# Causal mask by VectorE instead of a matmul, and sixteen biased exponentials for each of two sequences

## The reference

```python
x1 = x + attn(cond(x, labeler))           # cond: x @ W.T plus a low-rank term, chosen by a label per sequence
# attn: 32 heads of 32, 8 key/value heads, each shared by 4 heads
qkv = h @ w_qkv.T + b_qkv
q, k = apply_rope(q), apply_rope(k)
scores = einsum('bhqd,bhkd->bhqk', q, k) / sqrt(32)
scores = where(tril(ones(64, 64)), scores, -1e20)
attn = softmax(scores, axis=-1)
out = einsum('bhqk,bhkd->bhqd', attn, v) @ w_o.T + b_o
out2 = x1 + ffn(cond2(x1, language))      # two routed low-rank projections
```

## Time and profile before

| what | value |
|---|---|
| median of 3 runs | 1226.75 us (1225.2 to 1227.36) |
| span of the profiled execution | 1224.6 us |
| median less that span | 2.15 us |
| TensorE busy | 1199.6 us, 98% of the span |
| VectorE, ScalarE, GpSimd busy | 602.9, 379.0, 303.9 us |
| mean granted TensorE clock | 0.999 of full speed |

### The profile page before, as it was taken

How to read it: one execution, slowest core, us unless ns; L and a number is a source line. 1 busy time by engine, 2 the same in 40 slices (tenths; PEclk the granted TensorE clock), 3 DMA queues, 4 the chain that set the end, 5 groups by cost and what they waited for, 6 DMA issues and landing times.

```text
span 1224.6 us, 20268 instructions
## 1 busy us (share of the span) xinstructions
PE 1199.6 (98%) x7424; PEld 1071.1 (87%) x7440; DVE 602.9 (49%) x1173; ACT 379.0 (31%) x1157; POOL 303.9 (25%) x182
## 2 busy tenths in 40 slices
PE   7999999999999999999999999999999999999997
PEld 7999988888888888888889998888888888888886
DVE  5222136767676766777773226344443333334443
ACT  4212124455545555555543224111111111111110
POOL 0000123433433344444220002222222222222220
PEclk9999999999999999999999999999999999999999
DMA  6111032111111111110312314111111111111100
GB/s 245 35 36 51 9 121 82 44 47 56 43 48 46 43 43 43 43 52 25 119 54 87 108 70 139 53 59 59 52 51 51 51 51 51 51 51 51 51 35 34
DMA packets 30003, 74.82 MB, mean 61 GB/s; under 512 B 4114, under 2 KB 8722, under 8 KB 29970
## 3 DMA queue, kind: packets, MB, share of 16 engines
q1 hardware_dynamic: 29970, 74.36, 17.6%
HBM read 57.57 MB, written 16.78 MB: 61 GB/s over the span
## 4 chain that ended last, share of the span: by engine, by line
PE 93%; DVE 3%; ACT 1%; DMA 1%; issue 1%; POOL 0%; SPq 0%; DVEq 0%; ACTq 0%
PE psum L949 21%; PE psum L368 21%; PE psum L1499 19%; PE psum L1454 14%; PE psum L984 4%; PE psum L1012 4%; PE psum L1471 2%; PE psum L997 2%; PE psum L1479 2%; PE psum L968 1%; PE psum L1487 1%; PE psum L979 1%; PE psum L1029 1%; ACT low L738 1%; DVE rot_t L801 1%
## 5 line engine op out<-in xcount | busy, mean ns | idle before, releaser
L368 PE MATMUL psum<-c_high_low,w_h 128*128 128x256 f32 (+1 forms) x1344 | 238.4, 288 | 9.6 <-ACT w_h L242 8.1
L368 PEld LDWEIGHTS psum<-c_high_low,w_h 128*128 128x128 f32 x1344 | 205.0, 193 | 10.0 <-DVE c_high_low L296 8.1
L1499 PE MATMUL psum<-fr_h,c_high_low 128*128 128x512 f32 (+1 forms) x768 | 212.6, 361 | 0.1
L949 PE MATMUL psum<-p_h,c_high_low 128*128 128x512 f32 (+1 forms) x768 | 196.4, 359 | 0.5 <-DVE qkv L906 0.5
L368 PE MATMUL psum<-c_high_low,w_l 128*128 128x256 f32 (+1 forms) x704 | 177.8, 279 | 2.1 <-DVE w_l L350 2.1
L1454 PE MATMUL psum<-w_h,c_high_low 128*128 128x512 f32 x512 | 170.2, 397 | 0.8 <-DVE w_l L1279 0.8
L1499 PEld LDWEIGHTS psum<-fr_h,c_high_low 128*128 128x128 f32 x768 | 136.5, 188 | 22.6 <-issue 0.3
L949 PEld LDWEIGHTS psum<-p_h,c_high_low 128*128 128x128 f32 x768 | 134.1, 189 | 13.4 <-issue 0.7
L1499 PE MATMUL psum<-fr_l,c_high_low 128*128 128x512 f32 (+1 forms) x384 | 138.3, 360 | 0.0
L368 PEld LDWEIGHTS psum<-c_high_low,w_l 128*128 128x128 f32 x704 | 127.6, 193 | 2.3 <-DVE w_l L350 2.3
L1337 POOL TENSOR_TENSOR x_out<-x,spare 128x1024 f32<-128x1024 f32 x16 | 38.8, 2423 | 350.3 <-DMA out<-x_out 331.4
(11 more groups left out here) (142 smaller groups left out, 1996.5 us busy)
## 6 DMA issues: line engine op xcount, KB each, us to landing
ring<-in_x_t SPq DMA_DIRECT2D x32, 256.0 KB, 2.7
attn_scratch<-ring SPq DMA_DIRECT2D x16, 512.0 KB, 2.6
ring<-attn_scratch SPq DMA_DIRECT2D x32, 256.0 KB, 2.8
ring<-in_x_tok SPq DMA_DIRECT2D x16, 512.0 KB, 3.3
out<-x_out SPq DMA_DIRECT2D x16, 512.0 KB, 3.2
ring<-in_wqkv_t SPq DMA_DIRECT2D x12, 512.0 KB, 4.5
ring<-in_last_t SPq DMA_DIRECT2D x10, 512.0 KB, 4.8
w_raw<-in_w_cond SPq DMA_DIRECT2D x8, 512.0 KB, 9.4
```

What stands on the lines that cost most here:

```text
L368: mm = pe.matmul(to, stationary, moving, start=start and n == 0, stop=k == KT - 1 and n == len(passes) - 1, skip_group_check=True)
L949: mm = pe.matmul(to, sx[:, k, :], moving(w, n, k), start=first, stop=False, skip_group_check=True)
L1499: mm = pe.matmul(b_ps[:, n, 0:cols.stop - cols.start], s[:, k, :], w[:, k, cols], start=first, stop=n == 2 and k == KT - 1 and s is x1t_l)
```

## The change

VectorE now masks while it moves the scores out of PSUM: one `scalar_tensor_tensor` writes `-SCALE * scores - hidden`, where `hidden` (new, 128x64) holds 0 or -1e20, so hidden places come out at +1e20. A minimum over each 64 keys gives `shift`. ScalarE computes `exp(shift - value)` with `shift` as its bias. A bias belongs to one head's 64 columns, so this is 16 instructions of 64 columns for each sequence, all with their sums. The mask matmuls, their bf16 constants and VectorE's sum for sequence 1 go. On ScalarE the copies of the low-rank product stand among the exponentials of sequence 1: 8 exponentials, `down`, 3 more, `down_high`, the last 5, then `high_a` as before. VectorE's inverse sum of sequence 1 moves in front of the last of the three qkv additions.

```diff
-        def exp_scores(v, b, sums):
-            act.wait_ge(s_sub, 2 * v + b + 1)
-            if sums:
-                for g in range(2):
-                    for c in range(KVH):
-                        last = act.activation(prob[:, 0, g, c, :], prob[:, 0, g, c, :], ACT.Exp, scale=SCALE, accum_out=ssum[:, 0, g, c:c + 1])
-            else:
-                last = act.activation(prob[:, b, :, :, :], prob[:, b, :, :, :], ACT.Exp, scale=SCALE)
-            last.then_inc(s_exp, 1)
+        def exp_scores(v, b, first, last):
+            if first == 0:
+                act.wait_ge(s_shift, 2 * v + b + 1)
+            for n in range(first, last):
+                g, c = n // KVH, n % KVH
+                piece = act.activation(prob[:, b, g, c, :], prob[:, b, g, c, :], ACT.Exp, bias=shift[:, b, g, c:c + 1], scale=-1.0,
+                                       accum_out=ssum[:, b, g, c:c + 1])
+            if last == 2 * KVH:
+                piece.then_inc(s_exp, 1)
...
-                exp_scores(v, 0, main)
+                exp_scores(v, 0, 0, 16)
                 if not main:
                     fold2.high_w(act, 7)
-                exp_scores(v, 1, False)
+                exp_scores(v, 1, 0, 8)
             if main:
...
+                down(u)
+            if score:
+                exp_scores(v, 1, 8, 11)
+            if main:
+                down_high(u)
+            if score:
+                exp_scores(v, 1, 11, 16)
             if nxt:
                 high_a(act, u + 1)
                 high_x(act, u + 1, 1)
...
-        def inverse_sum(v, b, summed=False):
+        def inverse_sum(v, b):
             dve.wait_ge(s_exp, 2 * v + b + 1)
-            if not summed:
-                dve.tensor_reduce(row(ssum, b), flat(b), AX.X, ALU.add).then_inc(s_sum, 1)
...
             dve.reciprocal(row(sinv, b), row(ssum, b)).then_inc(s_inv, 1)
...
-                def less_max(b):
+                def masked(b):
                     dve.wait_ge(s_done, 2 * v + b + 1)
-                    dve.tensor_reduce(row(smax, b), scores, AX.X, ALU.max).then_inc(s_max, 1)
-                    dve.wait_ge(s_max, 2 * v + b + 1)
-                    dve.tensor_tensor(flat(b), scores, row(smax, b).unsqueeze(2).to_broadcast([P, 2 * KVH, SEQ]), ALU.subtract).then_inc(s_sub, 1)
+                    dve.scalar_tensor_tensor(flat(b), scores, -SCALE, hidden[:, :].unsqueeze(1).to_broadcast([P, 2 * KVH, SEQ]),
+                                             ALU.mult, ALU.subtract).then_inc(s_masked, 1)
+                    dve.wait_ge(s_masked, 2 * v + b + 1)
+                    dve.tensor_reduce(row(shift, b), flat(b), AX.X, ALU.min).then_inc(s_shift, 1)
...
                     dve.tensor_tensor(to, out[n] if n < NCH - 1 else psum[:, 2:4, 0:FCH], bias, ALU.add).then_inc(bank_out if n < NCH - 1 else qkv_out, 1)
+                    if score and n == NCH - 2:
+                        inverse_sum(v, 1)
...
             for g in range(2):
-                pe.matmul(s_ps[:, g, :], mask_l[:, :], mask_r[:, :], start=True, stop=False)
                 for q in range(QUADS):
...
-                                       start=False, stop=q == QUADS - 1 and n == 2)
+                                       start=n == 0, stop=n == 2)
```

More of the change, by code:

```diff
@@ L526, in attention @@
     prob = sb("prob", [P, BPU, 2, KVH, SEQ])
-    smax, ssum, sinv = (sb(n, [P, BPU, 2, KVH]) for n in ("smax", "ssum", "sinv"))
+    shift, ssum, sinv = (sb(n, [P, BPU, 2, KVH]) for n in ("shift", "ssum", "sinv"))
     pt_h, pt_l = (sb(n, [P, QUADS, 2, 2, P], F32R) for n in ("pt_h", "pt_l"))
@@ L533, in attention @@
     ident = sb("ident", [P, P])
-    mask_l = sb("mask_l", [P, P], BF16)
-    mask_r = sb("mask_r", [P, BANK], BF16)
-    mask_f = prob[:, 0, :, :, :].rearrange("p g c k -> p (g c k)")
+    hidden = sb("hidden", [P, SEQ])
     out = [psum[:, n, :].rearrange("p (o c) -> p o c", o=2) for n in range(2)] + [psum[:, 2, 0:FCH], psum[:, 3, 0:FCH]]
@@ L541, in attention @@
     low_ps = t_ps[:, 1, 0:P]
-    const_in, index_in, mask_ready = sem("const_in"), sem("index_in"), sem("mask_ready")
+    const_in, index_in = sem("const_in"), sem("index_in")
     x_in = [sem("x_in0"), sem("x_in1")]
@@ L554, in attention @@
     v_high, v_low, vb_zero, vb_high, vb_low = (sem(n) for n in ("v_high", "v_low", "vb_zero", "vb_high", "vb_low"))
-    s_done, s_max, s_sub, s_exp, s_sum, s_inv, s_norm = (
-        sem(n) for n in ("s_done", "s_max", "s_sub", "s_exp", "s_sum", "s_inv", "s_norm"))
+    s_done, s_masked, s_shift, s_exp, s_inv, s_norm = (
+        sem(n) for n in ("s_done", "s_masked", "s_shift", "s_exp", "s_inv", "s_norm"))
     pt_done, pt_high, pt_low = sem("pt_done"), sem("pt_high"), sem("pt_low")
@@ L559, in attention @@
     consts = [(b_bc[:, :], a["b_qkv"].partition_broadcast(P)), (cos[:, :], a["cos"]), (sin[:, :], a["sin"]),
-              (hmask[:, :], a["hmask"]), (ident[:, :], a["ident"]), (mask_f[:, BANK:BANK + P], a["mask_l"]),
-              (mask_f[:, 0:BANK], a["mask_r"])]
+              (hmask[:, :], a["hmask"]), (ident[:, :], a["ident"])]
+    consts += [(hidden[b * SEQ:(b + 1) * SEQ, :], a["mask_r"][0:SEQ, 0:SEQ]) for b in range(BPU)]
     def k_tiles():
@@ L669, in probs_high, with down, down_high @@
             act.activation(pt_h[:, :, :, :, :].rearrange("p q j g t -> p q (j g t)"), t_ps[:, :, :], ACT.Copy).then_inc(pt_high, 1)
-        def exp_scores(v, b, sums):
-            act.wait_ge(s_sub, 2 * v + b + 1)
-            if sums:
-                for g in range(2):
-                    for c in range(KVH):
-                        last = act.activation(prob[:, 0, g, c, :], prob[:, 0, g, c, :], ACT.Exp, scale=SCALE, accum_out=ssum[:, 0, g, c:c + 1])
-            else:
-                last = act.activation(prob[:, b, :, :, :], prob[:, b, :, :, :], ACT.Exp, scale=SCALE)
-            last.then_inc(s_exp, 1)
+        def exp_scores(v, b, first, last):
[7 more added lines that the diff above has]
+                piece.then_inc(s_exp, 1)
+        def down(u):
+            act.wait_ge(low_done, u + 1)
+            for b in range(BPU):
+                rows = slice(b * SEQ, (b + 1) * SEQ)
+                last = act.activation(low4[rows, :, :], down_ps[rows, b * LR:(b + 1) * LR].unsqueeze(1).to_broadcast([SEQ, 4, LR]), ACT.Copy, scale=LORA_SCALE)
+            last.then_inc(low_copied, 1)
+        def down_high(u):
+            act.wait_ge(low_t, u + 1)
+            act.activation(lows[:, :], low_ps, ACT.Copy).then_inc(low_high, 1)
         def step(u, main, score, value, nxt):
@@ L817, in row @@
             return t[:, b, :, :].rearrange("p g c -> p (g c)")
-        def inverse_sum(v, b, summed=False):
+        def inverse_sum(v, b):
             dve.wait_ge(s_exp, 2 * v + b + 1)
-            if not summed:
-                dve.tensor_reduce(row(ssum, b), flat(b), AX.X, ALU.add).then_inc(s_sum, 1)
-                dve.wait_ge(s_sum, UNITS + b if isinstance(v, int) and v == UNITS - 1 else v + 1)
             dve.reciprocal(row(sinv, b), row(ssum, b)).then_inc(s_inv, 1)
@@ L876, in step @@
                 scores = s_ps[:, :, :].rearrange("p g (c k) -> p (g c) k", k=SEQ)
-                def less_max(b):
+                def masked(b):
                     dve.wait_ge(s_done, 2 * v + b + 1)
-                    dve.tensor_reduce(row(smax, b), scores, AX.X, ALU.max).then_inc(s_max, 1)
-                    dve.wait_ge(s_max, 2 * v + b + 1)
-                    dve.tensor_tensor(flat(b), scores, row(smax, b).unsqueeze(2).to_broadcast([P, 2 * KVH, SEQ]), ALU.subtract).then_inc(s_sub, 1)
-                less_max(0)
+                    dve.scalar_tensor_tensor(flat(b), scores, -SCALE, hidden[:, :].unsqueeze(1).to_broadcast([P, 2 * KVH, SEQ]),
+                                             ALU.mult, ALU.subtract).then_inc(s_masked, 1)
+                    dve.wait_ge(s_masked, 2 * v + b + 1)
+                    dve.tensor_reduce(row(shift, b), flat(b), AX.X, ALU.min).then_inc(s_shift, 1)
+                masked(0)
                 if main:
-                    less_max(1)
-                    inverse_sum(v, 0, True)
+                    masked(1)
+                    inverse_sum(v, 0)
                 else:
@@ L891, in step @@
                     fold2.low_w(dve, 6)
-                    less_max(1)
-            if score and main:
-                inverse_sum(v, 1)
+                    masked(1)
             if main:
@@ L976, in scores @@
             else:
-                pe.wait_ge(s_sub, 2 * v + 1)
+                pe.wait_ge(s_masked, 2 * v + 1)
             for g in range(2):
-                pe.matmul(s_ps[:, g, :], mask_l[:, :], mask_r[:, :], start=True, stop=False)
                 for q in range(QUADS):
@@ L1004, in attend @@
                 pe.wait_ge(vb_low, v + 1)
-                pe.wait_ge(s_sub, 2 * v + 2)
+                pe.wait_ge(s_masked, 2 * v + 2)
             n = 0
@@ L1019, in transpose_down @@
                 pe.wait_ge(const_in, 16 * len(consts))
```

(1 more changed line is left out.)

2 lines of the change are left out of this document (removed).

## The result

The changed kernel takes 1284.24 us (median of 4 runs, 1282.77 to 1285.91) against 1226.05 before (4 runs, 1225.2 to 1227.36): a ratio of 1.0472, 95% interval 1.0457 to 1.0487. It is slower by 58 us. Forecast were 1287 us and the range 1244 to 1304.

What follows compares the result with a forecast made beforehand. TensorE, 93% of the span, was taken to bound the kernel before. Added to the profiled span, 51.8 us for steps 1 to 14, 2.6 for step 15 and 6.2 for step 16 (+60.6) led to 1287 us, range 1244 to 1304.

Steps and rivals of the forecast that it cites:

- What goes: TensorE in the loop: four mask matmuls of 0.23 us go from each unit, 0.93 us in 28.34.
- VectorE's pair: VectorE's two new instructions before ScalarE's exponentials: 2.51 us, as before; the scalar_tensor_tensor between 1.22 and 1.39 us.
- The exponential: Each new ScalarE exponential with a bias: 0.34 us instead of 0.24, bounds 0.24 and 0.355.
- forecast 3.7: Growth of one loop iteration in steps 1 to 14: 3.7 us, bounds 3.2 and 4.3.
- The queue behind the exponentials: ScalarE's low-rank copy 2.2 us late and `high_a` at 435.61 instead of 432.00, so TensorE's projection starts 3.4 later.
- The two waits that were forecast: TensorE in each iteration: 2.4 us for the low-rank copy, then 1.8 for the label matrix at the projection.
- The rotation behind `normalise`: VectorE's rotation due at 438.9 under GpSimd's `normalise` until 440.8; transposes start 3.7 us later.
- The ends: Steps outside the loop's 1 to 14: step 15 +2.6 us, step 16 +6.2, step 0 nothing.
- Step 16: Last step: the copy of sequence 0's transposed probabilities queues behind sequence 1's exponentials on ScalarE: +6.2 us.
- Step 15: No next label matrix: `up` 1.6 later, reciprocal 0.25, fold's low weight waiting up to 1.4: +2.6 us (1.9 to 3.3).
- The hidden fetch: Rival: ScalarE's bias fetch hides behind the accumulator's read, 0.24 us an exponential, +1.0 an iteration: 1244.6 us, chance 0.15.
- The clock: Rival: TensorE's clock falls in the new waits, 1.6 us lost each iteration, +22 in all: 1310 us, chance 0.10.

Runs made afterwards that it cites:

- e6: Kernel before with masking moved to VectorE's move of the scores, mask matmuls gone, no minimum made or subtracted, exponentials as before: 1211.94 us.
- e4: Changed kernel with the mask matmuls put back as matmuls of zeros, same shapes and place: 1292.08 us.
- e1: Changed kernel with only the bias operand of the exponentials taken away, so the softmax lacks its shift: 1247.06 us.
- e2: Kernel before with its sixteen exponentials of sequence 0 reading a per-partition bias of zeros: 1227.45 us.
- e3: Changed kernel with ScalarE's copies earlier: exponentials of sequence 1 go 1, 3, 3 and 9 around them instead of 8, 3 and 5: 1269.66 us.
- e7: As e3, with VectorE's inverse sum of sequence 1 moved behind the last of the three qkv additions: 1266.09 us.

## Why the prediction was right

**What goes.** 0.93 us an iteration for the masks: e6 gave 0.91. In the changed kernel the second half of it is hidden (e4).

**VectorE's pair.** Taken as 2.51 us between bounds; measured 2.51, the scalar_tensor_tensor of 1024 columns at 1.22 us, the lower bound.

**The exponential.** This was the term on which all hung. Forecast 0.34 us, with 0.10 for the operand from the `hmask` rows; measured 0.333, with 0.092 by e1 and e2. These runs agree with the 93 ns per pointer operand that the Trainium skill ("ScalarE: Activation LUTs", "What ACT_TABLE_LOAD costs") gives: 92 ns in both e1 and e2. My row, 113 ns, was 20 ns too high. Over 32 exponentials the 0.007 us between 0.34 and 0.333 are 0.2 us an iteration, and they account for forecast 3.7 against 3.50. That the operand is the larger part of the loss (37 of 58 us) is shown by e1; that the same operand costs nothing where the engine would have waited anyway, by e2.

**The queue behind the exponentials.** The two waits that were forecast are those of the trace, 2.1 us (forecast 2.4) and up to 1.4 (1.8). The first came in all of the steps 1 to 15, the second in nine and not in 14 or 15. The rotation behind `normalise` was forecast too: its first product took 1.83 us instead of 1.01, and ended at 466.95, 0.7 after `normalise` did (464.35 + 1.91). The same pair in e1, first GpSimd's instruction and then VectorE's:

```profile
444.70 1.90 POOL L775 TENSOR_TENSOR prob<-prob,sinv 128x1024 f32<-128x1024 f32 x1
...
444.88 2.40 DVE L808 TENSOR_TENSOR roped<-qkv,cos 128x640 f32<-128x640 f32 x1
```

It starts 0.18 us behind `normalise` and ends 0.68 after it. In the traces of all nine kernels the product starts 0.04 to 1.8 us after `normalise` in the steps of the loop, takes 0.82 to 2.55 us, and always ends 0.67 to 0.70 us after `normalise` does. So `normalise` sets its end, and with it GpSimd's queue behind `end_h`. In the changed kernel this costs little on top: behind the rotation TensorE waits 0.2 us for `pt_l`, 14 times, where I had forecast 0.3 (3.7 against 3.4).

**The ends.** Step 16 was forecast at +6.2 and measured +6.4. Step 15 is the term of the sum that was mis-sized: 2.6 against 5.3, outside its own bounds (1.9 to 3.3). The fold's first low weight did wait for `normalise`, and in full: VectorE's instruction took 2.60 us instead of 1.21. What was missing is the clock. Three stretches of the chain there:

```profile
649.67 2.05 PE psum L954 x6
...
666.39 2.19 PE psum L1016 x12
668.57 1.70 PE psum L973 x8
```

and the same before:

```profile
601.86 1.16 PE psum L949 x6
...
616.01 1.43 PE psum L1012 x12
617.44 0.87 PE psum L968 x8
```

Behind TensorE's wait of 2.1 us for `low` the granted clock was 0.50 from 650 to 653, and behind its wait of 2.9 us for the fold's next low weight (until 665.17) again 0.50 from 667 to 670. Nothing hid either: 0.9 and 1.6 us, 2.5 of the 2.7 that the forecast lacks. The +1.2 us behind step 16 are the clock for the most part too. The last six large matmuls of the program, in this execution and in that of before:

```profile
1277.30 2.61 PE L1482 MATMUL psum<-c_high_low,lb_h 128*128 128x512 f32 x6 [0.76 <-DVE lb_h L1403]
```

```profile
1219.19 1.66 PE L1479 MATMUL psum<-c_high_low,lb_h 128*128 128x512 f32 x6 [0.76 <-DVE lb_h L1400]
```

They ran at 0.50 now and at 1.00 before, 1.0 us; the start, taken as 0, gave 2.8 back. The errors cancel in part: 51.8 + 2.6 + 6.2 = 60.6 was forecast, 59.1 came. That the sum is 1.5 us off and no more is luck: the loop and the start came out 2.8 each below it, step 15, step 16 and what follows 4.1 above it.

**The hidden fetch** (1244.6 us, chance 0.15) is what e1 made of the kernel, at 1247. With the operand, the exponentials lay 0.333 us apart in the changed kernel and in e2, so none of the fetch was hidden by the accumulator's read.

**The clock.** It did fall, and the rival's price for that in the loop (1.6 us an iteration) was wrong. Two successive iterations of the changed kernel as windows (clock, DMA share and GB/s at the end):

```profile
473.44:505.30 31.86, 27.89 (x179) 24.73 (x177) 20.02 (x28) 20.79 (x89) 11.39 (x7) 1.00 0.11 41
441.59:473.44 31.85, 29.16 (x178) 25.96 (x177) 19.29 (x28) 20.90 (x89) 11.39 (x7) 0.95 0.12 41
```

In 9 of steps 1 to 14 the granted clock went to 0.50 (1.2 GHz) behind the wait for `low`, for a little over three us. Those iterations are as long as the other five, since TensorE then only reaches later the label matrix that it would have waited for, and since the rotation ends with `normalise` however late VectorE gets to it. The half clock ate the second wait (in four of the nine 0.4 us of it is left, as at 463.29, in five nothing) and cost nothing. In e3 the fall comes at another place, where no wait follows:

```profile
427.00:428.00 1.00, 0.77 (x3) 0.77 (x4) 0.89 (x2) 0.63 (x2) 1.00 (x1) 0.57 0.44 133
...
429.00:430.00 1.00, 1.00 (x7) 1.00 (x6) 1.00 (x3) 0.00 (x0) 0.00 (x0) 0.50 0.00 0
430.00:431.00 1.00, 1.00 (x8) 1.00 (x8) 1.00 (x3) 0.00 (x0) 0.89 (x1) 0.72 0.00 0
```

There the distance to the next iteration is 31.70 instead of 30.46. All four long distances of e3 begin in such a fall, and so do the three of e7 (31.41 and 31.42 instead of 30.47); none of the others does. So in a loop one fall costs 0, 0.95 or 1.2 us, by what follows it. What sets whether the clock falls is not settled: the same wait of 2.11 us was followed by a fall in nine steps and by none in five.

What stays open besides: how the 21 us of e1 divide between the number of exponentials and their order. In the same place, e3's other order took 15 us off with the operand left in.

## What to carry to other kernels

An instruction's price counts where a queue makes others wait for it: ask of each added instruction what stands behind it on its engine and who waits for that, down to the second and third waiter. A bias for each 64 columns turned 17 exponentials into 32, each of 64 columns 92 ns dearer, and held up two copies and a matrix that had nothing to do with the softmax. Work taken off the engine that bounds a loop is worth its full time only as long as that engine stays the bound (0.91, 0.42 or 0.25 us of the same 0.93 here).

## What the runs showed of the hardware

- A per-partition bias on an exponential of 64 columns with accumulator output adds 92 ns (243 to 335 between e1 and the changed kernel, 242 to 334 between the kernel before and e2), both in the record and in the distance to the next (0.24 to 0.333 us).
- The scalar_tensor_tensor of 1024 columns from PSUM, with a broadcast second operand, takes 1.22 us, no more than the reduction (1.22) or the subtraction of before.
- A VectorE product of two SBUF tensors (128x640, 0.81 us by itself) that starts during a GpSimd instruction ended 0.67 to 0.70 us after that instruction, whether it had started 0.04 or 1.8 us behind it (all nine kernels).
- A fall of TensorE's clock to its lower level behind a wait cost nothing where another wait followed (nine steps of the changed kernel, waits of 2.1 us), and 1.2 us (e3, waits of 2.2) or 0.95 us (e7, waits of 1.6) where none did.
